# A graph network on one core: layer 2's one-hots in PSUM, earlier one-hots in layers 0 and 1, ScalarE's copies ahead of laying out in layer 1, 24 picks for 22 in layer 0

## The reference

```python
# layer 0
m = relu(x[src] + edge_attr_32);  y = (1 + eps) * x + segment_sum(m, dst)
# layer 1 (cosine attention)
e = beta * sum(norm(x)[src] * norm(x)[dst]);  p = softmax of e over the edges of one dst
y = segment_sum(x[src] * p, dst)
# layer 2 (spline convolution, 5 x 5 kernel weights, 4 corners an edge; note: summed by src)
h[src, corner] += basis * x[dst];  y = einsum(h, weight) / degree + x @ root + bias
# layer 3: five rounds of a PNA layer (sum, mean and maximum over the edges of one dst)
x = layernorm(x + y)          # after each of the four
```

## Time and profile before

| | |
|---|---|
| Median of 3 runs | 12678.07 us (12668.12 to 12689.16) |
| The profiled execution | 12666.39 us, span 12664.3 us |
| Busy: PE, PEld | 11319.6 us (89%), 10240.8 us (81%) |
| Busy: DVE, ACT, POOL | 8190.9 us (65%), 6690.6 us (53%), 8860.0 us (70%) |
| Mean granted TensorE clock | 0.942 of 2.4 GHz |
| Picks of layer 0 | 174.7 to 1441.2 us |
| Picks of layer 1 | 1645.2 to 3228.0 us |
| Matmuls of layer 2 | 3483.4 to 6104.0 us |
| Layer 3 | from 6184 us to the end |

### The profile page before, as it was taken

One profiled execution on the slowest core, in us unless ns is written; L12 is line 12 of the kernel. 1 busy time (PEld: TensorE's weight loads), 2 busy tenths in 40 slices (PEclk: granted clock), 3 DMA queues, 4 the chain that ended last, 5 costly groups with the idle time before them and its releaser, 6 DMA issues. The chain is left out here.

```text
span 12664.3 us, 161164 instructions
## 1 busy us (share of the span) xinstructions
PE 11319.6 (89%) x59997; PEld 10240.8 (81%) x59997; DVE 8190.9 (65%) x11332; ACT 6690.6 (53%) x6601; POOL 8860.0 (70%) x8316
## 2 busy tenths in 40 slices
PE   4999568888799999999899989998999899989997
PEld 4888457777488899998788878887888788878886
DVE  4666545665377888888666656665666566656666
ACT  1333233333378888887455545554555455545554
POOL 4777655555388888888577767776777677767776
PEclk9999789898599999999899989998999899989998
DMA  6332222222222222222122222222222222222222
GB/s 196 92 92 90 47 46 60 57 56 60 84 76 80 78 81 77 78 81 76 53 87 83 88 61 88 82 89 62 85 87 83 65 85 86 83 70 81 84 86 68
DMA packets 591091, 1001.27 MB, mean 79 GB/s; under 512 B 173310, under 2 KB 433019, under 8 KB 572011
## 3 DMA queue, kind: packets, MB, share of 16 engines
q1 hardware_dynamic: 284075, 702.46, 15.4%
q0 software_dynamic: 290784, 295.40, 11.7%
q10 hardware_dynamic: 15936, 0.65, 0.1%
HBM read 621.40 MB, written 418.90 MB: 82 GB/s over the span
## 5 line engine op out<-in xcount | busy, mean ns | idle before, releaser
L1957 POOL DMA_INDIRECT l3g<-TQ,srcs x4480 | 4463.3, 996 | 1635.8 <-issue 1029.8
L2075 PE MATMUL ps<-qs,oh 128*128 128x384 f32 (+1 forms) x26880 | 5540.0, 360 | 0.0
L2075 PEld LDWEIGHTS ps<-qs,oh 128*128 128x128 f32 x26880 | 4878.0, 190 | 76.9
L2239 DVE TENSOR_REDUCE l3g<-ps 128x32 f32<-128x416 f32 x3360 | 1917.7, 584 | 2045.6 <-PE ps L2075 2026.9
L1826 PE MATMUL ps<-l2mm,l2oh 128*128 128x408 f32 (+1 forms) x12544 | 2439.7, 355 | 197.9 <-DVE l2mm L1898 197.9
L2162 ACT CAST oh<-nd 128x1536 fp32r<-128x1536 bf16 x1120 | 1653.7, 1477 | 1737.0 <-DVE nd L2235 1737.0
L1810 POOL DMA_INDIRECT l2g<-Y,place x1568 | 2139.3, 1364 | 616.9 <-issue 477.4
L1826 PEld LDWEIGHTS ps<-l2mm,l2oh 128*128 128x128 f32 x12544 | 2343.2, 190 | 277.2 <-DVE l2mm L1898 235.6
L1898 DVE TENSOR_TENSOR l2mm<-l2hl,l2m 128x1768 fp32r<-128x1768 f32 x784 | 1512.8, 1993 | 22.5 <-PE ps L1826 18.4
L1841 ACT ACTIVATE l2oh<-l2far,l2one 128x512 fp32r<-128x512 f16 x1568 | 1134.6, 724 | 514.8 <-PE ps L1826 512.4
L1272 POOL DMA_INDIRECT l1g<-T,srcs x896 | 854.9, 954 | 727.2 <-DVE l1g L1506 543.9
(11 more groups left out here) (352 smaller groups left out, 8891.7 us busy)
## 6 DMA issues: line engine op xcount, KB each, us to landing
W<-l3o SPq DMA_DIRECT2D x140, 1792.0 KB, 5.8
mneg<-KG SPq DMA_DIRECT2D x280, 384.0 KB, 3.4
l3g<-TQ,srcs POOLq DMA_INDIRECT x4480
l3t<-AT SPq DMA_DIRECT2D x140, 448.0 KB, 3.9
W<-l1o SPq DMA_DIRECT2D x28, 952.0 KB, 4.4
l0e<-U_a SPq DMA_DIRECT2D x28, 896.0 KB, 4.6
S<-RX SPq DMA_DIRECT2D x49, 512.0 KB, 4.9
W<-l0e SPq DMA_DIRECT2D x28, 896.0 KB, 3.7
```

The source lines that it names most:

```text
L1957: e.indirect_dma_start(G3[s][:, j, :], None, TQ, bass.IndirectOffsetOnAxis(ap=srcs[:, c * C + j:c * C + j + 1], axis=0)).then_inc(z3[f"g{s ...
L2075: x_ = e.matmul(ps[k % 3][:, 0:32 * n], OH[k // SB][:, g, 128 * (k % SB):128 * (k % SB) + 128], QS[:, p, 32 * n0:32 * (n0 + n)], start=Fal ...
L2239: e.tensor_reduce(G3[r // KP % 3][:, C - KP + r % KP, :], ps[r % KP % 3][:, 0:32 * PH].rearrange("p (h f) -> p f h", f=32), AXX, ALU.max). ...
```

## The change

Four things are changed, and no arithmetic but the type of `M5`.

1. Layer 0 picks 24 columns of a chunk and gathers 32; its blocks are of 12 columns, and `SPREAD0` makes the one-hots behind takes 0, 2, 4 and 6 of 12 (before: 2, 4, 6, 8 of 11).
2. Layer 1's `SPREAD1` makes them behind takes 0, 1, 2 and 3 of 8. ScalarE's list is reordered so that all four `widen`s of a block stand together, but for `exps` and `spread` that stand around the first of the second block; `lay`, `lays` and `fm` come after.
3. `M5` lies in PSUM banks 6 and 7 as float32.
4. Each gather of layer 2 from the 29th on waits until `by_h` has gone through all but the last 26 or so of the columns before it.

```diff
-KP0 = 22
-SB0 = 11
+KP0 = 24
+SB0 = 12
-SPREAD0 = ((), (), (0,), (), (1,), (), (2,), (), (3,), (), ())
+SPREAD0 = ((0,), (), (1,), (), (2,), (), (3,), (), (), (), (), ())
-SPREAD1 = ((), (0,), (), (1,), (), (2,), (), (3,))
+SPREAD1 = ((0,), (1,), (2,), (3,), (), (), (), ())
...
-            M5 = [sb(ph, f"l2m5_{i}", [128, C2, 2, PH], BF16) for i in range(2)]
+            M5 = [ps[6 + i][:, 0:2 * C2 * PH].rearrange("p (c k h) -> p c k h", k=2, h=PH) for i in range(2)]
...
             for c in range(NCH):
-                widen(NB1 * c + 1, 0)
-                widen(NB1 * c + 1, 1)
+                for g in range(PG):
+                    widen(NB1 * c + 1, g)
                 if c:
                     exps(c - 1)
-                widen(NB1 * c + 1, 2)
+                widen(NB1 * c + 2, 0)
                 if c:
                     spread(c - 1)
-                widen(NB1 * c + 1, 3)
-                widen(NB1 * c + 2, 0)
+                for g in range(1, PG):
+                    widen(NB1 * c + 2, g)
                 if c:
                     lay(c - 1)
                 e.wait_ge(z1["sl"], 16 * (c + 1))
                 e.copy(V1[:, 0:32, 1:C + 1].rearrange("p f j -> p j f"), S1[:, :, :]).then_inc(z1["lays"], 1)
-                for g in (1, 2, 3):
-                    widen(NB1 * c + 2, g)
                 if c:
                     e.wait_ge(z1["filled"], c)
...
                 for j in range(C2):
+                    if j0 + j >= 2 * C2:
+                        e.wait_ge(*z2.at("mk", (j0 + j) // 2 - C2 + 1))
                     e.indirect_dma_start(G2[s3][:, j, :], None, cells,
```

## The result

The changed kernel took 12160.6 us (median of 4 runs, 12152.8 to 12161.6) where the kernel before took 12673.1 us in the same comparison: a ratio of 0.960, 95% interval 0.9585 to 0.961. The profiled execution took 12152.8 us against 12666.4 us, 513.6 us less. 12205 us had been forecast.

A forecast was written before the change was run, and what follows sets the result against it. GpSimd was taken to bound layers 2 and 0, the handing on of one-hots layer 1. Gains of 225 (layer 2), 220 (layer 1) and 25 us (layer 0), 470 in all, gave 12205 us, range 12050 to 12400.

The forecast's parts named there:

- (a): Layer 2: `M5` in PSUM as float32 leaves `by_h` as fast; costed at nothing, covered by VectorE's 2.4 us of slack.
- (d): Layer 2: TensorE sets the period, 21.4 us a block where it was 23.4, winning 225 us (180 to 240).
- Step (b): Layer 2: gathers beside `by_h` drop from 1.61 to 0.94 us, the mean to 1.05; GpSimd drops below TensorE.
- step (c): Layer 2: the gathers' new wait on products leaves GpSimd about 13 us to spare.
- The walk: Layer 1: one chunk followed on VectorE; TensorE waits of 0.8, 0.4, 1.6 and 2.6 us make it 46.4 us.
- The last term: Layer 1: half clock expected after the 2.6 us wait alone, taking a chunk from 46.4 to 48.5 us.
- keys in time: Layer 1 rival, 17%: key rows land in 3 us instead of 6, or waits are overestimated; 44 us a chunk, 12085 us.
- The rival on the other side: Layer 2 rival, 4%: `by_h` is slow from PSUM and VectorE becomes the bound; 13510 us at twice the product's time.

The follow-up runs named there:

- one half alone: The kernel before with only ScalarE's new order in layer 1, VectorE's one-hots left behind takes 1, 3, 5, 7: 12713.6 us, 1.0045.

## Why the prediction was right, and where it was off

**The bounds were named rightly.** GpSimd bound layers 0 and 2, ScalarE's late copies layer 1. After the change TensorE is the bound of layers 0 and 2, as forecast, and the experiments on the parts give each layer its own gain.

**Layer 2, steps (a) to (d): right.** `by_h` 1.992 us (forecast: no change), gathers 1.019 us (1.05), 2398 us for the layer (2400), 21.4 us a block. The 1.05 us was borrowed from layer 0 and not worked out, and nothing hung on it: by an estimate from the same rows, a mean gather of up to 1.23 us (21.4 / 14 less 0.30) would still have left TensorE the bound. Step (b) took the 1.61 us for the price of a gather beside `by_h`; it is the time to the product's end and 0.8 us more. The comparison on which step (b) rested, one gather beside a product with a PSUM operand in another layer, held, though the products and the index rows differed. That the memory and not the type does it was only assumed in the forecast; the float32 run in SBUF shows it. Of step (c), the run without the gate shows that the gate costs nothing; that 13 us are to spare wasn't measured.

**Layer 1: mechanism right, size 34 us low.** The walk gave waits of 0.8, 0.4, 1.6 and 2.6 us; 0.62, 0.34, 1.19 and 2.55 came, and VectorE's waits came as 1.92 us for `spread` (1.9) and 4.38 us for the key rows (4.7). Chunk: 41.0 + 4.7 + 1.6 for the clock = 47.3 us, where 48.5 was forecast and 47.5 measured. The largest miss among the waits is the one behind the late key rows, by 0.4 us; the others were 0.2, 0.1 and less than 0.1 us too large. The last term, half clock after the fill alone, was sized at 2.1 us and measured 1.6 us. That it follows the fill's wait came true for 24 of 26 such waits here; with `spread` moved forward it is 5 of 26, so the length of the wait alone doesn't decide it. The gain was also taken times 27 chunks, where 27.95 count. Of the rivals, "keys in time" described a kernel that had to be made: with the key rows ahead of the store the layer runs at 43.9 us a chunk, where the rival said 44.

**Layer 0: right for half a wrong reason.** 44.3 us a chunk against 44.5. The pick was priced at up to 1.71 us, from layer 1, and costs 1.62 us; and the forecast credited the earlier places with shortening a wait. With 22 picks they shorten none (1.0000). What went is the 0.69 us wait for a take, and that only with 24 picks. The 44.5 us were chosen between 43.3 and 45.3 and not worked out, so the match is in part luck; so is that of 25.5 with 25, as the picks before vary by 12 us between profiled kernels.

**The rest:** 11 us came outside the three loops, mostly from layer 0's end to layer 1's first pick (204.0 to 195.2 us), for which nothing was forecast. It belongs to layer 0's part: the stretch takes 192 to 197 us in every profiled kernel with that part, and 204 to 208 us in every one without it. What shortens it stays open.

**The rival on the other side** (`by_h` slow from PSUM) is out: 1992, 1994 and 1993 ns. The 62 cycles more that the Trainium skill (VectorE: DVE Perf Modes, The TRN2 errata) gives a PSUM source, an estimate of 0.065 us a product, don't show in this product with one source in PSUM and one in SBUF either.

## What to carry to other kernels

When GpSimd's gathers bound a loop, look at what VectorE reads beside them: a product with both operands in SBUF held each gather until the product's end here, 1.61 us for 0.95, and moving one small, often re-read operand to PSUM gave that back at no cost to the product. An order of work that two engines share is one edit, not two: one half alone lost 55 us where both won 254. And when waits for one thing go, walk the chunk for the next ones; here three small causes (a store ahead of a load in a queue, a copy ahead of a needed one, one scan of 4 us) were worth another 1.4% together.

## What the runs showed of the hardware

**Half clock after short waits.** In the changed kernel 24 of the 26 waits of 2.55 us in layer 1 come with a stretch at 1.2 GHz (granted 0.50; 0.57 over the 4 us shown), in which two picks take 2.75 and 2.25 us instead of 1.71. Over four profiles it is 101 of 104 such waits when 1.0 to 1.75 us of idle time lies shortly ahead, and 5 of 26 waits of 2.39 to 2.56 us, in the experiment with `spread` first, when at most 0.67 us lies there. Neither the length of the wait nor the idle time ahead of it decides every case. In layer 1 waits of 129 us in sum cost some 38 us more by the clock, and each edit that took away one of their causes won 1.4 to 1.7 times what the waits alone were worth (102 us for 63, 91 for 54, 98 for 69).

**A gather is held by a VectorE operation with two inputs in SBUF.** A gather that starts while such an operation runs ends some 0.8 us after that operation's end (777 of 820 beside `by_h` in the kernel before, 0.80 to 0.84 us), so it took 1.59 to 2.77 us beside `by_h` and up to 1.87 us beside the message steps, against 0.95 us alone or beside a product with one operand in PSUM. The exceptions start within 0.02 us of the operation itself. What the engines share there, the runs don't show; that the place of one operand decides, they do.
